# A linear-attention scan taken two steps at a time, and the stage before it reordered

## The reference, cut to what matters

```python
# layer 0, end of the mixture: the two chosen experts' rows, weighted, and the residual
out = jnp.einsum('blkd,blk->bld', expert_rows, combine_weights)
x = x + gb * out
h = _layernorm(x) * (1 + ca) + sa            # input of layer 1's attention
# layer 1, linear attention: 16 heads, 16 keys and 32 values each, 512 time steps
gk = jax.nn.log_sigmoid(h @ Wgk1 @ Wgk2 + bgk2) / 16
def step(S, inp):                            # S: b, head, 16, 32
    qt, kt, vt, gt = inp
    S = S * jnp.exp(gt)[..., None] + kt[..., None] * vt[..., None, :]
    ot = jnp.einsum('bhk,bhkv->bhv', qt, S)
    return (S, ot)
o = o * jax.lax.rsqrt(jnp.mean(o * o, -1, keepdims=True) + EPS) * norm_w
o = o * (g * jax.nn.sigmoid(g))
```

## Time and profile before

| | us |
|---|---|
| median of the runs shown | 2705.67 |
| the profiled execution, its own time | 2707.49 |
| its span, first to last instruction | 2705.8 |
| stage before the scan | 1662.4 to 1782.0 |
| the scan, with its fill and drain | 1782.2 to 2251.9 |

### The profile page before, as it was taken

One profiled execution on the slowest core, in us unless ns is written; L12 is line 12 of the kernel. 1 busy time (PEld: TensorE's weight loads), 2 busy tenths in 40 slices (PEclk: granted clock), 3 DMA queues, 4 the chain that ended last, 5 costly groups with the idle time before them and its releaser, 6 DMA issues. The chain is left out here.

```text
span 2705.8 us, 34528 instructions
## 1 busy us (share of the span) xinstructions
PE 2421.2 (89%) x10120; PEld 1639.4 (61%) x10120; DVE 1763.3 (65%) x2613; ACT 1279.9 (47%) x2550; POOL 1100.3 (41%) x1112
## 2 busy tenths in 40 slices
PE   6999979999999996989999994669898876999999
PEld 5778845555555553857888883435444424788877
DVE  4230239999999995786555553669989997511253
ACT  3223039999999994235555552742223213411121
POOL 0112035666666663672000002358988995111110
PEclk9999989999999997989999997889999998999999
DMA  5254445555555554668767764534444455201021
GB/s 181 81 134 171 121 105 168 161 171 175 158 171 171 162 158 137 230 226 269 227 229 230 229 218 148 195 127 155 173 156 162 169 179 170 79 24 47 12 87 65
DMA packets 287527, 421.45 MB, mean 156 GB/s; under 512 B 37817, under 2 KB 120777, under 8 KB 287409
## 3 DMA queue, kind: packets, MB, share of 16 engines
q1 hardware_dynamic: 252656, 369.16, 43.0%
q10 hardware_dynamic: 28704, 33.08, 3.6%
q0 software_dynamic: 6048, 17.75, 2.0%
HBM read 304.11 MB, written 115.82 MB: 155 GB/s over the span
## 5 line engine op out<-in xcount | busy, mean ns | idle before, releaser
L1068 ACT ACTIVATE attn_probs<-attn_ps_score,attn_nmax 128x512 f32<-128x512 f32 x512 | 342.8, 674 | 2.2 <-DVE attn_nmax L1142 2.2
L2635 PE MATMUL scan_ps_o<-scan_qs,scan_sel 128*128 128x512 f32 x512 | 266.1, 637 | 83.2 <-DVE scan_qs L2579 61.8
L2597 DVE TENSOR_TENSOR_SCAN scan_st<-scan_ps_dec,scan_kv 128x512 f32<-128x512 f32 x256 | 305.8, 1209 | 9.4 <-POOL scan_kv L2549 9.3
L975 PE MATMUL attn_ps_score<-attn_KK,attn_X 64*128 64x512 f32 x512 | 214.1, 466 | 20.7 <-ACT attn_probs L1068 20.2
L2635 PEld LDWEIGHTS scan_ps_o<-scan_qs,scan_sel 128*128 128x128 f32 x512 | 89.0, 194 | 230.7 <-DVE scan_qs L2579 152.2
L1156 DVE SCALAR_TENSOR_TENSOR attn_mixed<-attn_probs,attn_cf,attn_mixed 128x512 f32<-128x512 f32 x256 | 192.4, 752 | 9.1
L1131 DVE TENSOR_REDUCE attn_raw<-attn_ps_score 128x2 f32<-128x1024 f32 x128 | 156.4, 1222 | 29.8 <-PE attn_ps_score L975 28.7
L975 PE MATMUL attn_ps_score<-attn_KL,attn_X 64*128 64x512 f32 x512 | 172.3, 422 | 0.0
L87 POOL MEMSET head_ident<- 128x128 f32 x1 | 0.2, 203 | 410.9 <-POOLq L3286 410.9
L2549 POOL TENSOR_TENSOR scan_kv<-scan_vb,gla_gk 128x512 f32<-128x512 f32 x128 | 160.8, 1281 | 11.8 <-DMA scan_vb<-gv 4.9
L975 PE MATMUL attn_ps_score<-attn_KK,attn_Y 64*128 64x512 f32 x512 | 160.0, 398 | 0.8 <-POOL attn_Y L865 0.8
(11 more groups left out here) (559 smaller groups left out, 6809.4 us busy)
## 6 DMA issues: line engine op xcount, KB each, us to landing
scan_vb<-gv SPq DMA_DIRECT2D x256, 256.0 KB
moe_raw<-in_L_ffn_gating SPq DMA_DIRECT2D x92, 512.0 KB, 4.5
rows_x<-attn_zeros SPq DMA_DIRECT2D x32, 1024.0 KB, 13.5
moe_raw<-in_L_ffn_linear SPq DMA_DIRECT2D x46, 512.0 KB, 4.6
late<-rows SPq DMA_DIRECT2D x32, 384.0 KB, 8.9
attn_spread<-rows SPq DMA_DIRECT2D x32, 384.0 KB
moe_xb<-rows_x SPq DMA_DIRECT2D x23, 512.0 KB, 4.8
rows_y<-moe_y ACTq DMA_DIRECT2D x23, 512.0 KB, 6.6
```

Source lines behind the costliest of these rows:

```text
L975: last = nc.tensor.matmul(ps_score[n][:, j, :], weights, y[p][half, :], start=(r == 0), stop=(r == len(terms) - 1))
L1068: nc.scalar.activation(probs[b][:, at_j, :], ps_score[n][:, j, :], ACT.Exp, bias=nmax[b][:, at_j:at_j + 1], accum_out=Z[b][:, at_j:at_j + ...
L2597: V.tensor_tensor_scan(st[r][:, :], ps_dec[n % 2][:, :], kv[r][:, :], 0.0, ALU.mult, ALU.add).then_inc(st_ready, 1)
L2635: nc.tensor.matmul(ps_o[w][:, :], sel[:, P - GPH - GPH * d:2 * P - GPH - GPH * d], qs[i % RING][:, :], start=(d == 0), stop=(d == HALF - 1 ...
```

## The change

In the scan:

- A step of GpSimd's `kv` and of VectorE's scan now covers two values: 128x1024. The decay lies twice in `ps_dec` (two PSUM banks), with a zero at the first element of the second copy, so that one scan instruction starts anew in the middle. `kv` and `st` are rings of 3 pairs, `qs` a ring of 2 pairs.
- VectorE's weighing covers the pair (k = 2), or its first half where GpSimd weighs the second (k = 1). What waited for a step now waits for a pair, except that each half of `qs` is waited for by itself.
- The sums have one PSUM bank, so TensorE waits at each 16 values until ScalarE has taken the 16 before. The root goes to SBUF (`osq[:, 1, :]`) instead of PSUM.
- On ScalarE an evacuation stands three steps later than its tile and the root two; `logs`, the log-sigmoid and `decay` stand four steps later, `finish` at j = 10 and `gate` at j = 12.
- The first eight loads of `vb` are issued at the end of the stage before; the constants are written behind the first `kv`; the two loads of `norm_w` go out at i = 16.

In the stage before: GpSimd gathers the rows of two half batches first and then writes the constants; each tile's gather has a semaphore of its own; `y1` and `y2` lie in `vb`. SyncE loads x and the gate first and waits for the gathered rows before it issues most of the weights. ScalarE and VectorE split only the first weight chunk ahead of the mixing, and more of them in batches 1 and 2. In batch 3 the last two evacuations stand behind `shifted`.

```diff
-        FINISH_AT = 8
+        FINISH_AT, TILE_LATE, SQUARES_LATE = 10, 3, 2
...
-        LOG_AT, LESS_AT, DECAY_AT, SQUARES_AT = 14, 24, 30, 3
+        LOG_AT, LESS_AT, DECAY_AT, SQUARES_AT = 18, 28, 34, 3
...
+            def weigh_second(m_):
+
+                i = 2 * m_ + 1
                 b, h = divmod(i // NV, HG)
-                pool.wait_ge(st_ready, i + 1)
-                if i >= RING:
-                    pool.wait_ge(summed, i - RING + 1)
-                G.tensor_tensor(qs[r][:, :], st[r][:, :], gq[b % 2][:, h, :], ALU.mult).then_inc(pool_qs_ready, 1)
-
-            for i in range(NB * NV):
+                pool.wait_ge(st_ready, m_ + 1)
+                pool.wait_ge(summed, i - RING + 1)
+                G.tensor_tensor(qs[m_ % WEIGHED_PAIRS][:, 1, :], st[m_ % PAIRS][:, T:], gq[b % 2][:, h, :], ALU.mult
+                                ).then_inc(pool_qs_ready, 1)
...
-                pool.wait_ge(v_in[i % AHEAD], (i // AHEAD + 1) * 16)
-                if i >= RING:
-                    pool.wait_ge(st_ready, i - RING + 1)
-                G.tensor_tensor(kv[r][:, :], vb[i % AHEAD][:, :], gk[b % 2][:, h, :], ALU.mult).then_inc(kv_ready, 1)
-                if 1 <= i < 2 * (P // GPH):
-                    one_diagonal(i - P // GPH)
-                if i >= 2 and by_pool(i - 2):
-                    weigh(i - 2)
+                for y in (i, i + 1):
+                    pool.wait_ge(v_in[y % AHEAD], (y // AHEAD + 1) * 16)
+                if m_ >= PAIRS:
+                    pool.wait_ge(st_ready, m_ - PAIRS + 1)
+                y = i % AHEAD
+                G.tensor_tensor(kv[m_ % PAIRS].rearrange("p (y t) -> p y t", t=T), vb[:, y:y + 2, :], gk[b % 2][:, h, :].unsqueeze(1).to_broadcast([P, 2, T]),
+                                ALU.mult).then_inc(kv_ready, 1)
...
+                if m_ and by_pool(i - 1):
+                    weigh_second(m_ - 1)
...
+                k = 1 if by_pool(i + 1) else 2
+                dve.wait_ge(st_ready, m_ + 1)
+                dve.wait_ge(q_copied, i // NV + 1)
                 if i >= RING:
-                    dve.wait_ge(summed, i - RING + 1)
-                V.tensor_tensor(qs[r][:, :], st[r][:, :], ps_q[:, :], ALU.mult).then_inc(qs_ready, 1)
+                    dve.wait_ge(summed, i - RING + k)
+                V.tensor_tensor(qs[m_ % WEIGHED_PAIRS][:, :k, :], st[m_ % PAIRS][:, :k * T].rearrange("p (y t) -> p y t", t=T),
+                                ps_q[:, :].unsqueeze(1).to_broadcast([P, k, T]), ALU.mult).then_inc(qs_ready, 1)
...
+                    weighed(dve, i - 2 * PAIRS)
+                    weighed(dve, i - 2 * PAIRS + 1)
+                V.tensor_tensor_scan(st[m_ % PAIRS][:, :], ps_dec[n % 2][:, :], kv[m_ % PAIRS][:, :], 0.0, ALU.mult, ALU.add).then_inc(st_ready, 1)
+                if m_:
+                    weigh(m_ - 1)
...
-                if d == 0 and n:
-                    pe.wait_ge(o_ready, n * 2 - 1 + w)
-                nc.tensor.matmul(ps_o[w][:, :], sel[:, P - GPH - GPH * d:2 * P - GPH - GPH * d], qs[i % RING][:, :],
+                if d == 0 and i:
+                    pe.wait_ge(o_ready, n * 2 + w)
+                nc.tensor.matmul(ps_o[:, :], sel[:, P - GPH - GPH * d:2 * P - GPH - GPH * d], qs[i // 2 % WEIGHED_PAIRS][:, i % 2, :],
...
-                nc.scalar.activation(ps_rstd[:, :], lnms, ACT.Exp, scale=-0.5).then_inc(rstd_ready, 1)
+                nc.scalar.activation(rstd, lnms, ACT.Exp, scale=-0.5).then_inc(rstd_ready, 1)
...
+                for r in at_step.get(i - TILE_LATE, ()):
+                    if items[r][0] != "ms":
+                        evacuate(r)
+                for r in at_step.get(i - SQUARES_LATE, ()):
```

More of the change, by code:

```diff
@@ L2124, in mixture_and_inputs @@
             "dec_ready"))
-        gathered, g_in, v_stored = ([m.sem(f"{n}{p}") for p in two] for n in ("gathered", "g_in", "v_stored"))
+        gathered = [[m.sem(f"gathered{p}_{t}") for t in range(PER)] for p in two]
+        g_in, v_stored = ([m.sem(f"{n}{p}") for p in two] for n in ("g_in", "v_stored"))
         raw_in = [m.sem(f"raw_in{p}") for p in range(RAWS)]
@@ L2181, in _ @@
                         load_x(q + 4)
+            for p in two:
+                sp.wait_ge(v_stored[p], 32)
+            gv = s["gv"][0].rearrange("(g v h) t -> g v h t", g=HG, h=GPH)[0]
+            for v_ in range(len(s["v_in"])):
+                sp.dma_start(s["gvb"][:, v_, :], gv[v_].unsqueeze(1).to_broadcast([GPH, DK, T])).then_inc(s["v_in"][v_], 16)
             for q in range(4):
@@ L2314, in _ @@
                 normalised(b)
-                if b:
-                    for i in range(GROUP * b - 2, GROUP * b):
-                        evacuate(i)
+                if b == 0:
+                    for n in range(TT, TT + PER):
+                        weigh(n)
+                late = range(GROUP * b - 2, GROUP * b) if b else ()
+                for i in late if b < B - 1 else ():
+                    evacuate(i)
                 if b == 2:
@@ L2322, in _ @@
                 shifted(b)
+                for c in (next(later), next(later)) if b == 0 else ():
+                    high(c)
+                for i in late if b == B - 1 else ():
+                    evacuate(i)
             for p in two:
@@ L2381, in log_sigmoid @@
                                        ).then_inc(ls_ready, 1)
-            for c in range(EARLY_LOW):
-                low_weights(c)
-            later = iter(range(EARLY_LOW, NC))
+            low_weights(0)
+            later = iter(range(3, NC))
             for b in range(B):
@@ L2390, in _ @@
                         low(b - 1)
-                    for _ in range(1 if b == 0 else 0 if t < 2 else 2):
+                    for _ in range(2 if b and t >= 1 else 0):
                         for c in later:
@@ new lines, in _ @@
+                if m_ >= PAIRS:
[3 more added lines that the diff above has]
+                                ALU.mult).then_inc(kv_ready, 1)
+                if m_ == 0:
+                    constants()
+                for y in (i, i + 1):
+                    if 2 <= y < 2 * (P // GPH) + 1:
+                        one_diagonal(y - 1 - P // GPH)
@@ L3360, in build @@
                 s["gbias"], s["gone"] = m.sb("bias", [P, HG]), m.sb("one", [P, 1])
+                s["gvb"], s["v_in"] = m.sb("vb", [P, 8, T]), [m.sem(f"v_in{i}") for i in range(8)]
                 mixture_and_inputs(nc, a, s, x1, x2)
```

160 lines of the change are left out of this document (83 added, 77 removed).

## The result

Six runs of the changed kernel have a median of 2729.32 us (2721.52 to 2736.53), six of the kernel before 2705.68: a ratio of 1.0073, 95% interval 1.0056 to 1.009. It is slower, by 15 to 24 us, and above the forecast range, which ended at 2721. The profiled execution took 2729.08, 21.6 more than that of before.

| us | before | after | difference | forecast |
|---|---|---|---|---|
| up to the stage before the scan (code not touched) | 1662.4 | 1668.8 | +6.4 | 0 |
| the stage before the scan | 119.8 | 119.8 | 0.0 | -3 |
| start of the scan to the first scan | 7.7 | 2.5 | -5.2 | -5.3 |
| first to last scan | 448.7 | 463.3 | +14.6 | +6.8 |
| last scan to the last store | 13.3 | 17.0 | +3.7 | +3.3 |

A forecast was written before the change was run, and what follows sets the result against it. The prediction took VectorE, GpSimd and TensorE to bound the scan at once, near 6.26 us per four steps. Its terms, led by +18.8 for the loop and -13.4 for q's copy, summed to +1.8: 2707.5, rounded 2708, range 2685 to 2721.

The forecast's parts named there:

- Part 2: Scan quads (four steps) with a TensorE tile: waiting on sums slows each from 6.26 to 6.83 us, 33 quads, +18.8.
- the loop: GpSimd's weighing waits for TensorE's sums and tile, VectorE's scan for the `kv` behind it: 13.66 us for two quads.
- Part 4: Finishing and gating: finishing multiplications +1.4 us, VectorE's wait for `kv` behind the gating +10.5, log-sigmoid -2.5.
- Part 1: Longer scan instructions: scan pairs 2.20 us, GpSimd's pairs 2.38, VectorE's quad of four steps 6.09 against 6.26.
- rival B: Scan: the loop does not bind, tile quads run at TensorE's 6.26; Part 2 and Part 3 fall away, -21.5, 2684; chance 0.27.
- Part 3: One PSUM bank for the sums: TensorE waits for the copy every 16 values, +4.5 us, between 0 and 9.
- false floor: In scan quads with a tile, TensorE was read as needing 6.26 us for four sums and the tile.
- rival E: Finishing multiplications starve, each waiting behind a whole `kv` pair if GpSimd runs late: +15 us, 2723; chance 0.12.
- Part 5: ScalarE's new order in the scan: VectorE's waits for q's copy go, -13.4 us, and for the root, -8.5.
- Part 6: Start and end of the scan: earlier first load -5.3 us, constants delaying the second pair +1.7, longer end +3.3.
- Part 7: Stage before the scan: gathering rows first lets batch 0 normalise earlier; -3 us carried through, between +1 and -8.

The follow-up runs named there:

- Experiment 7: One projection tile of each batch computed twice, filling TensorE's idle stretch behind the gating, against the changed kernel: 2718.42 us, 1.0029 of the kernel before.
- experiment 5: The gating split into two halves two steps apart, against the changed kernel: 2710.82 us, 1.0003 of the kernel before.
- experiment 1: One slot more for what GpSimd weighs, so it waits for the sum of step i-8 instead of i-4, against the changed kernel: 2690.58 us, 0.9928 of before.

## Why the prediction was wrong

**The step that failed is Part 2's price of the loop**, "From the moment at which VectorE has weighed ... 6.83 each", taken as the same in every turn and priced with TensorE at its full clock. Its mechanism and its plain turn are right (13.70 against 13.66). But Part 4's wait behind the gating and Part 2's loop were added as if they knew nothing of each other, and the clock stood in no term. That wait leaves TensorE idle for 3.3 to 3.8, the clock falls to half, and the next turn goes through the slow sums: 15.4 (once 16.4) instead of 13.7 in each of five groups. Experiment 7 took the fall away in three of them by giving TensorE work, and experiment 5 shows one group without it.

The size comes from VectorE's waits for `kv` in groups 1 to 5, where all of this lies. They are 48.5 (summed from its rows); the forecast's terms hold 37.4 there: 33 x (6.83 - 6.09) for the loop, 4.5 for the bank, 5 x 1.7 for the gatings. The 11.1 between them are three differences:

- The clock, forecast at nothing, costs 10.6 by these comparisons: 5 x 1.65 = 8.3 in the dear quads, 0.7 in group 4 where it stays down longer, and 1.6 at the sixth fall in group 2 (a wait of 3.0 where the same place of group 4 has 1.4).
- The waits behind the gating are 3.2, 1.9, 3.2, 1.9 and 3.2, 13.4 in all: 4.9 more than forecast. In experiment 1, without the loop, they are 1.9 to 2.0 in all groups, so the loop adds to them too.
- The waits that are left, the loop's own and the bank's, are 24.5 instead of 28.9: 4.4 less.

The other terms, from their own runs:

- Part 1: pairs 2.285 and 2.38, quads without a tile 6.09: right. The reading that TensorE needs 6.26 in a tile quad was wrong (6.09 in experiment 1). Experiment 1 is rival B made true: its scan is 19.0 below before, where B's terms give 16.5 (6.8 less 23.3).
- Part 2 and Part 3 together: 23.3 forecast. After less experiment 1 is 33.6, of which 33 x 0.17 = 5.6 is the false floor. The remaining 28.0 hold the clock as well, 10.9 by the quads of this profile (5 x 1.65, 1.05 and 1.6), and lack 3.4 by which the log-sigmoid is shorter in after than in experiment 1. That leaves 20.5 for the 23.3. Experiment 1 has falls of its own, at 1914 and 1924 in group 2, which takes 59.5 where its group 4 takes 55.4; with these 4.1 it would be 24.6. One profile of each tells no more.
- The bank alone is 4.2 between the two profiles, whose falls of the clock are not the same: near the forecast's 4.5, not confirmed to the us.
- Part 4: finishing multiplications 1.4 to 1.6 a pair, so rival E did not happen; the wait behind the gating is 1.9 in groups 2, 4, 6 and 7, but 3.2 in groups 1, 3 and 5. The log-sigmoid takes 4.5 in all three where it took 11.7: forecast -2.5, measured -7.2. Part 4's reading that it gets its data when GpSimd first pauses does not hold after the change. GpSimd has no gap there, yet the log-sigmoid ends 1.1 behind the pair that was running when it started (1962.10 to 1964.47), and the next pair takes 3.35 instead of 2.38:

```profile
1964.10 1.46 DVE L2620 SCALAR_TENSOR_TENSOR gla_gdec<-gla_gdec,gla_gsg 128x1024 f32<-128x1024 f32 x1
...
1962.10 5.68 POOL L2578 TENSOR_TENSOR scan_kv<-gla_vb,scan_gk 128x1024 f32<-128x1024 f32 x2
```

So it waited for one instruction alone, the possibility that Part 4 names and sets aside. In experiment 1 it starts 0.24 behind the start of a pair instead of 2.0 and takes 3.2, again until 1.1 behind that pair's end. Why it had to let three more instructions pass before the change stays open.

- Part 5: no wait for q and none for the root in groups 0 to 6: right. By itself the order is worth 16.5 of scan rather than 21.9, mainly since VectorE then waits 6.5 more for `kv`.
- Part 6: -5.2 for -5.3, and +3.7 for +3.3: right.
- Part 7 forecast -3 and got 0 (119.8 both times). Batch 0 does normalise earlier (23.7 behind the stage's start instead of 34.1), but the end does not move. Eleven profiles with the new stage take 117.2 to 120.2, two with the old one 119.8 and 120.1. What takes the gain back was not tried.

Outside of the changed stages the two profiles differ by 8.3. Of this, 6.4 is the time at which the untouched part ends; over the thirteen profiles it lies between 1659.7 and 1669.5, with 1662.6 and 1668.8 both in versions with single steps, so it is no effect of the change that these runs could show. The medians leave 3 to 7 us more than the 13.1 of the changed stages (ratios 1.0059 and 1.0073); whether that is the spread of the untouched stages or something small and real stays open.

Over the whole program the profile lies 19.8 above the forecast (21.6 for 1.8). The scan makes 7.8 of it, which are the 11.1 of waits in groups 1 to 5 and 1.7 of waits in the others, less 4.7 for the log-sigmoid, to 0.3. Part 7's -3 that did not come is 3.0, the untouched stages are 8.3, start and end 0.5, to 0.2 in all. On the profile's own scale the changed stages alone make 2707.5 + 13.1 = 2720.6, the last of the range; without the clock's 10.9 it would have been 2710. So whether the time fell in or out of the range hung on the untouched stages, which the forecast says nothing about; the step above was wrong either way. The range was narrow above because each rival priced one mechanism, and none let one mechanism change another's price.
